# Two edits at once in a four-layer graph kernel: attention weights read from PSUM in three edge passes, and the third edge pass on table rows of three bf16 parts

## What is computed

```
layer 0 (4 heads of 32, edge types):  a_e = (kw[src] . q[dst]) * pri / sqrt(32)
                                      att = exp(a_e - max over dst) / sum over dst;  agg = sum over dst of msg[src] * att
layer 1 (4 heads of 32):              a_e = leaky_relu(a_src[src] + a_dst[dst], 0.2), softmax over dst, sum of xh[src] * alpha
layer 2:                              h = relu(norm(x)) * clip(out_degree, 1) ** -0.5
                                      agg = sum over dst of h[src];  relu((agg @ W) * clip(in_degree, 1) ** -0.5 + b)
layer 3 (8 heads of 16):              s = exp(clip(K[src] . Q[dst] / 4, -5, 5))
                                      (sum of V[src] * s) / (sum of s + 1e-6), then a dense part with two batch norms
```

## Time and profile before

| | |
|---|---|
| median of three executions | 10693.53 us |
| the profiled execution | 10696.8 us |
| its span | 10695.1 us |
| mean granted TensorE clock, share of full speed | 0.631 |
| busy: POOL | 7984.3 us (75%) |
| busy: PE | 6694.1 us (63%) |
| busy: PE weight load | 5319.6 us (50%) |
| busy: DVE | 5218.1 us (49%) |
| busy: ACT | 2509.1 us (23%) |

### The profile page before, as it was taken

How to read it: one execution, slowest core, us unless ns; L and a number is a source line. 1 busy time by engine, 2 the same in 40 slices (tenths; PEclk the granted TensorE clock), 3 DMA queues, 4 the chain that set the end, 5 groups by cost and what they waited for, 6 DMA issues and landing times. The chain is left out here.

```text
span 10695.1 us, 165052 instructions
## 1 busy us (share of the span) xinstructions
PE 6694.1 (63%) x38290; PEld 5319.6 (50%) x38291; DVE 5218.1 (49%) x13802; ACT 2509.1 (23%) x6808; POOL 7984.3 (75%) x11114
## 2 busy tenths in 40 slices
PE   4977777777756667666663333333337777777776
PEld 3656665655535555555553232232224555555554
DVE  4266666666665555555553111111114555555555
ACT  1333333333343333333333000000002111111111
POOL 0188888888848888888865666666663888888884
PEclk9966666676765555555556555565556666666667
DMA  3333333333312212222111222222222332333332
GB/s 112 148 88 88 87 87 87 87 88 88 87 46 47 46 44 46 45 46 45 44 40 46 46 46 46 47 46 46 46 46 63 87 87 87 87 87 87 87 87 63
DMA packets 379652, 731.26 MB, mean 68 GB/s; under 512 B 169770, under 2 KB 219233, under 8 KB 373126
## 3 DMA queue, kind: packets, MB, share of 16 engines
q0 software_dynamic: 251264, 621.88, 22.1%
q1 hardware_dynamic: 100762, 97.56, 2.8%
q10 hardware_dynamic: 27500, 10.39, 0.4%
HBM read 652.50 MB, written 76.88 MB: 68 GB/s over the span
## 5 line engine op out<-in xcount | busy, mean ns | idle before, releaser
L465 POOL DMA_INDIRECT edges_rows<-conv_rows,edges_idx_r x1568 | 1536.9, 980 | 773.6 <-issue 457.9
L465 POOL DMA_INDIRECT edges_rows<-gat_rows,edges_idx_r x1568 | 1562.8, 997 | 336.1 <-issue 260.1
L465 POOL DMA_INDIRECT edges_rows<-kv_typed,edges_idx_r x1568 | 1597.6, 1019 | 267.6 <-issue 263.5
L465 POOL DMA_INDIRECT edges_rows<-kv_rows,edges_idx_r x1568 | 1522.2, 971 | 271.6 <-issue 267.7
L1022 PE MATMUL edges_ps_sum<-edges_rows,edges_pick 128*128 x3520 | 763.3, 355 | 1511.7 <-issue 1386.9
L629 PE MATMUL edges_ps_sum<-edges_wv,edges_pick 128*128 128x132 f32 x7040 | 1671.9, 409 | 20.9 <-issue 13.4
L472 POOL TENSOR_TENSOR edges_pause<-edges_pause 128x56 f32<-128x56 f32 x4704 | 1599.9, 340 | 108.1 <-issue 18.1
L629 PEld LDWEIGHTS edges_ps_sum<-edges_wv,edges_pick 128*128 128x128 f32 x7040 | 1427.0, 297 | 256.6 <-issue 246.5
L1022 PEld LDWEIGHTS edges_ps_sum<-edges_rows,edges_pick 128*128 128x128 f32 x3520 | 647.9, 257 | 1627.1 <-issue 1625.7
L1120 PE MATMUL edges_ps_q<-q,edges_pick_t 128*128 x3520 | 748.7, 379 | 674.5 <-DVE edges_prod L1184 649.7
L1042 DVE TENSOR_TENSOR sums<-sums,edges_ps_sum 128x129 f32 x440 | 126.9, 288 | 1858.5 <-DMA edges_rows<-gat_rows,edges_idx_r 1486.5
(11 more groups left out here) (345 smaller groups left out, 10934.8 us busy)
## 6 DMA issues: line engine op xcount, KB each, us to landing
kv_typed<-l0pre_out SPq DMA_DIRECT2D x49, 1024.0 KB
edges_rows<-kv_typed,edges_idx_r POOLq DMA_INDIRECT x1568
edges_rows<-gat_rows,edges_idx_r POOLq DMA_INDIRECT x1568
edges_rows<-conv_rows,edges_idx_r POOLq DMA_INDIRECT x1568
edges_rows<-kv_rows,edges_idx_r POOLq DMA_INDIRECT x1568
edges_feat_r<-visit_features ACTq DMA_DIRECT2D x660, 10.0 KB
kv_rows<-l3pre_kv SPq DMA_DIRECT2D x7, 896.0 KB
edges_flag_r<-visit_flags ACTq DMA_DIRECT2D x220, 16.0 KB
```

Source lines behind the costliest of these rows:

```text
L465: pool.indirect_dma_start(rows[:, k, g * width:(g + 1) * width], None, table, bass.IndirectOffsetOnAxis(ap=idx_r[:, k, g:g + 1], axis=0)). ...
```

## The change

It has four parts, made together.

- In the first, second and fourth pass ACT takes the exp a second time, into a PSUM bank `ps_weight`: once for a span of four visits (128x64) in the first two, once per visit (128x32) in the fourth, each after the `weigh` that last read that bank. `weigh` takes its second operand from there. The exp into `wv` stays, since the sums need it.
- In the first pass `make_pick` reads its iota from a PSUM bank, filled once.
- Of the banks, the first pass has one bank `ps_near` and not two, so that `squares` runs two visits ahead and not three and waits for the ACT instruction that read the bank last; `ps_turn` goes into the same bank as `ps_top`, so that `turn_logits` waits for the last reader of the block's maxima (`gap_b`). The fourth pass has two `ps_near` and not three, and `squares` runs three ahead and not four.
- The third pass works on rows of three bf16 parts, high, mid and low, whose sum is the float32 number, and the one: 385 numbers, 770 bytes. The one-hot matrix is bf16, PE takes four bf16 matmuls of 385 columns per visit, and DVE adds the three parts to the sums one after the other. The parts are made on POOL in `conv_inputs`: four instructions of 128x896 for each of seven sets of node tiles, behind POOL's seven memsets; the table is stored when the low part is cut.

```diff
 # softmax_pass, DVE weigh (L815) and make_pick (L772)
-            nc.vector.tensor_tensor(wv4[:, s % 3, :, :, 0:hd], vals, bcast(wv4[:, s % 3, :, :, hd], [P, G, heads, hd]),
-                                    ALU.mult).then_inc(wv_done, 1)
+            j = s % SPAN
+            weights = ps_weight[:, j * GH:(j + 1) * GH].rearrange("p (g h) -> p g h", g=G)
+            nc.vector.tensor_tensor(wv4[:, s % 3, :, :, 0:hd], vals, bcast(weights, [P, G, heads, hd]), ALU.mult).then_inc(wv_done, 1)
...
-                                            c["iota_bf"].unsqueeze(1).broadcast_to([P, G, P]),
+                                            ps_iota[:, 0:P].unsqueeze(1).broadcast_to([P, G, P]),
 # softmax_pass, ACT weigh_gap (L671)
                     if s % SPAN == 0:
                         act.wait_ge(gap_done, t * 3 + s // SPAN + 1)
+                        if known(u, 1):
+                            act.wait_ge(wv_done, u)
+                        nc.scalar.activation(ps_weight[:, 0:SH], gap[:, s // SPAN, :], ACT.Exp).then_inc(span_weighed, 1)
 # softmax_pass, banks and PE
-        ps_near = [p.ps(f"ps_near{j}", [P, GE]) for j in range(near_banks)]
+        ps_near = p.ps("ps_near", [P, GE])
-        ps_turn, ps_top = p.ps("ps_turn", [P, 512]), p.ps("ps_top", [P, 512])
+        ps_top, ps_weight = p.ps("ps_top", [P, 512]), p.ps("ps_weight", [P, 512])
+        turned_top = ps_top[:, 0:P]
...
                     if known(w, 1):
                         pe.wait_ge(ends_done, w)
+                        pe.wait_ge(gap_b, w)
-                    nc.tensor.transpose(ps_turn[:, 0:P], logit[:, r, :], c["ident"]).then_inc(turn_done, 1)
+                    nc.tensor.transpose(turned_top, logit[:, r, :], c["ident"]).then_inc(turn_done, 1)
...
-                    if known(u, near_banks):
-                        pe.wait_ge(pick_tb_done, u + 1 - near_banks)
+                    if known(u, 1):
+                        pe.wait_ge(pick_tb_done, u)
...
-                    to_square, to_spread, last, ninth = (wide_at(i, k, it, d) for d in (3 if dot else 2, 1, -1, -9))
+                    to_square, to_spread, last, ninth = (wide_at(i, k, it, d) for d in (2, 1, -1, -9))
 # clipped_pass, ACT (L1151) and DVE weigh (L1191)
                         act.wait_ge(gap_done, u + 1)
+                        if known(u, 1):
+                            act.wait_ge(wv_done, u)
+                        nc.scalar.activation(ps_weight[:, 0:G * heads], gap[:, s % 3], ACT.Exp).then_inc(gap_weighed, 1)
...
-                                            bcast(wv4[:, w, :, :, hd], [P, G, heads, hd]), ALU.mult).then_inc(wv_done, 1)
+                                            bcast(ps_weight[:, 0:G * heads].rearrange("p (g h) -> p g h", g=G), [P, G, heads, hd]),
+                                            ALU.mult).then_inc(wv_done, 1)
 # conv_pass (L976)
-        rows = p.sb("rows", [P, SLOTS, G * aw])
+        rows = p.sb("rows", [P, SLOTS, G * PARTS], BF16)
-                        mm = nc.tensor.matmul(ps_sum[k % banks][:, 0:aw], pick[:, k % deep, g * P:(g + 1) * P], now[:, g, :],
+                        mm = nc.tensor.matmul(ps_sum[k % banks][:, 0:PARTS], pick[:, k % deep, g * P:(g + 1) * P], now[:, g, :],
-                    nc.vector.tensor_tensor(blk, blk, ps_sum[k % banks][:, 0:aw], ALU.add).then_inc(acc_done, 1)
+                    nc.vector.tensor_tensor(blk[:, 0:D], blk[:, 0:D], ps_sum[k % banks][:, D:2 * D], ALU.add).then_inc(mid_done, 1)
+                    dve.wait_ge(mid_done, u + 1)
+                    nc.vector.tensor_tensor(blk, blk, ps_sum[k % banks][:, 2 * D:PARTS], ALU.add).then_inc(low_done, 1)
+                    dve.wait_ge(low_done, u + 1)
+                    nc.vector.tensor_tensor(blk[:, 0:D], blk[:, 0:D], ps_sum[k % banks][:, 0:D], ALU.add).then_inc(acc_done, 1)
 # conv_inputs (L1695), SP and POOL
-                    sp.wait_ge(row_done, (k + 1) * CH)
+                    sp.wait_ge(low_cut, k + 1)
...
+                for k in range(SETS):
+                    row = table[:, k % 2]
+                    high, mid, low = (parts[:, k % 2, :, n * D:(n + 1) * D] for n in range(3))
+                    pool.wait_ge(row_done, (k + 1) * CH)
...
+                    nc.gpsimd.tensor_copy(high, row).then_inc(high_cut, 1)
+                    pool.wait_ge(high_cut, k + 1)
+                    nc.gpsimd.tensor_tensor(rest_rows[:], row, high, ALU.subtract).then_inc(high_off, 1)
+                    pool.wait_ge(high_off, k + 1)
+                    nc.gpsimd.tensor_copy(mid, rest_rows[:]).then_inc(mid_cut, 1)
+                    pool.wait_ge(mid_cut, k + 1)
+                    nc.gpsimd.tensor_tensor(low, rest_rows[:], mid, ALU.subtract).then_inc(low_cut, 1)
```

81 lines of the change are left out of this document (44 added, 37 removed).

## The result

The changed kernel took 11248.77 us (median of four, 11229.03 to 11259.24) against 10694.37 us: ratio 1.0513, 95% interval 1.0498 to 1.0528. It is 5% slower, where 10440 us was forecast.

The account below looks back on a forecast made before the run. POOL was taken to bound the edge passes, the fullest engine in each. Fourth -130, first -55, second -15, third -70 and dense part +15 sum to -255 us, giving 10440 us; range 10220 to 10610.

Parts of the forecast that it names:

- What bounds the kernel: All four edge passes: POOL is the fullest engine; in the fourth, consumers follow it with 0.70 us of waiting per visit.
- Fourth pass, -130: Fourth pass: POOL's stretched pauses and DMAs shrink once weigh reads PSUM; -130 us, ends -138 and 0.
- First pass, -55: First pass: of 154 us excess on POOL, half of DVE's 111.8 us wait is gained; ends +20 and -154.
- Second pass, -15: Second pass: DVE's loop counts, weigh gets shorter, a faster POOL only waits more; -15 us, ends +20 and -75.
- Third pass, -70: Third pass: bf16 halves PE's matmul records, so fewer of POOL's 243 us of slot waits; -70 us, ends 0 and -243.
- the creep: Third pass: PE at times runs slowly, 18.3 us per visit, then catches up, while POOL's slots fill.
- by records: Third pass: creep goes by matmul records, halved to 4 per visit; a visit takes 9.2 us, gain -79 us.
- by entries: Third pass: creep goes by all PE queue entries, about 25 per visit before, 17 after; 12.4 us per visit, -38 us.
- Dense part before it, +15: Before the third pass: POOL cuts rows into parts, 1.7 us per instruction taken; +15 us, between +8 and +25.
- E: First two passes: fewer banks and the weight handshake chain PE, ACT and DVE; +308 us, 10820 us in all; chance 0.05.
- D: Pauses are stretched by DVE's broadcast operand and stay; only the third pass moves, 10640 us; chance 0.05.
- The rules of the skill: Two weighed: SBUF-SBUF products shouldn't delay indirect DMAs (first pass 62 us at most); PSUM sources add 65 ns per product, 114 us.

Follow-up runs that it names:

- e2: Changed kernel with weigh and make_pick reading both operands from SBUF again, third pass with a 56-column pause; ratio 1.0181 to the kernel before, chip 1.
- f1: The kernel before, unchanged, run on chip 10 for its trace: 11042 us.
- g1: The kernel before, unchanged, run on chip 11 for its trace: 10300 us.
- e4: Kernel before with POOL's pause cut from 56 to 4 columns in first, second and fourth pass, same pause added in the third; ratio 1.0761, chip 1.

## Why the prediction was wrong, point by point

- **What bounds the kernel: half right.** POOL does set the pace, and the stretched instructions are where it said. The step that failed is in the fourth pass: "the consumers follow POOL and have slack to follow a faster one". The 0.70 us of waiting per visit were read as slack that doesn't depend on POOL. On the chip of the result and on chips 1 and 10 they do: with DMAs 1.43 us apart throughout, PE's signals come late, DVE waits for them 296 us before L1200 alone, the slack is gone, and POOL waits 180 us for `weigh`. The sum has no term for this, in this pass or in the other two with pauses.
- **Fourth pass, -130:** measured +40, and -134 on chip 11, where PE is on time. The term was right for a chip without late signals.
- **First pass, -55:** measured +329, and -116 on chip 11. The bound by DVE's 111.8 us of waiting was itself a symptom: in the earlier trace rows's pass ACT had already 460.3 us of "remote" waits before L679, which I had not followed up, and the same instruction of the same kernel waits 300.5 us for rows on chip 11. There the consumers keep up and 116 of the 154 us come.
- **Second pass, -15:** measured +96, and -10 on chip 11. POOL's wait for `weigh` did grow, as said (70 to 202 us), but not because a faster POOL only waits more: PE was late.
- **Third pass, -70:** measured +8. Both accounts of the creep (by records, by entries) are refuted: PE's matmuls halved, and POOL's waits for slots went from 243 to 252 us. The 1386.9 us of "issue" were not all creep either: on chip 11, with all records, the same matmuls of the kernel before are idle for 1122.9 us, 1060.7 of them waiting for POOL. Where there is no creep the pass takes 1974 us before and 1981 after: bf16 rows are worth nothing to it.
- **Dense part before it, +15:** measured +12, and +15 on chip 11; the casts took 1.02 and 0.94 us for 1.7, the differences 1.83 each.
- **Rivals.** E had the sign, with a wrong mechanism: e2 shows its banks and waits at no cost in the first pass and at most 16 us in the second, where it put 0.35 us per visit, and on chip 11 the kernel that has them all is faster. D and its broadcast operand are out, since the pauses fell to their floor. What came was named nowhere in the prediction, although its own rows showed PE running 24 matmuls in 55 us beside DMAs 1.25 us apart, and no such creep in the passes with pauses. "Passes with far more PE work show no creep and so records are not the cause" should have gone on: what those passes have and this one lacks is the pause. They weren't free of the trouble, as the "remote" waits show.
- **The rules of the skill.** The row disagreed with the inference of the Trainium skill, "SBUF — State Buffer", section "Who interferes with whom", and now the runs do: with both SBUF-SBUF products gone the first pass's DMAs fell from 1019 to 962 ns, and with them back (e2) rose to 1020. So such a product does delay an indirect DMA on GpSimd, and on chip 11 the same pair goes from 1023 to 962 ns. The 65 ns per product that the Trainium skill, "VectorE: DVE Perf Modes", section on the TRN2 errata, would add for a PSUM source did not come: `weigh` took 676 ns with its PSUM operand, 711 before (682 where its record is shortest in the fourth pass before, 678 with PSUM on chip 11).

**What stays open:** why PE is late. The runs show that it depends on the distance of POOL's DMAs and on the chip, and not on banks, handshakes or (with the reservation above) the rows per DMA. Whether the matmuls or their signals are late, and what path they share with the DMAs, no run shows. Nor do the runs give one average distance at which PE turns late: in the first pass of e2 it is late at 1.533 us without any wait of POOL for `weigh`. Where between 1.43 and 1.53 us on average POOL begins to wait in the first and fourth pass of chip 1 isn't measured. No version beat the kernel before on a chip with late signals.

**A rival that no run tests** is the recording itself. The packed trace of the kernel before holds 114942 records of a DMA raising a semaphore on chip 11, but 36491 in the trace that the prediction read and 35062 on chip 10, for the same program. The view of DMAs shows it, first of f1 (chip 10), then of g1 (chip 11): only where the records are complete does it give the time from issue to landing (2.8 us).

```profile
edges_rows<-kv_typed,edges_idx_r POOLq DMA_INDIRECT x1568
edges_rows<-kv_typed,edges_idx_r POOLq DMA_INDIRECT x1568, 2.8
```

The traces of the result and of chips 1 and 10 lack 49 to 72% of these records, those of chips 8 and 11 less than 1%, so the missing records and the late signals are found on the same chips. Every time on record comes with a recorded span and clock, so the runs don't tell whether PE is late, or the changed kernel slower, when nothing is recorded.

## What to carry to other kernels

A wait of a consumer for its producer is slack only as long as the consumer's own speed doesn't depend on the producer's rate: before a gain on the pacing engine is booked, shorten a pause (one number, as in e4) and see whether the rest follows. Waits called "remote" on one core mean that a signal came late; count them before counting instructions. "issue" can be a plain wait whose record is missing: see first whether the trace is complete, that is, whether its DMAs have a time to landing. And a tuned pause can hold for one chip alone: the same pair of kernels differs by +6.2% on one chip and -2.3% on another, so a change of this kind is to be timed on several.

## What the runs showed that was not expected

- The same kernel before takes 10300, 10693 or 11042 us by the chip, with PE's clock alike (means of 0.62 to 0.64). The difference lies in the first three passes, where PE's signals are late; the fourth takes about 2394 us in each of its three traces.
- A pause of POOL shorter by 0.08 us in three passes (with the same short pause in the third) made that kernel 7.6% slower on chip 1.
- Two indirect DMAs without an instruction between them have 0.30 us of issue, with one 0.16 us: a pause of 0.21 us costs the third pass only some 0.11 us per DMA (2137 for 1961 us, both on chip 8).
